# Cross attention with two score slots a batch, and a feed-forward that turns values still carrying their rounding constant

## The chip, the cores and the metric

The kernel runs on one core of a Trainium2 chip. A core has a matrix engine (TensorE, PE in the profile; its weight loads are listed apart as PEld), a vector engine (VectorE, DVE), an activation engine (ScalarE, ACT), a general engine (GpSimd, POOL) and a sync engine (SyncE, SP) that here only issues DMAs. Each engine runs its own list of instructions in order; the engines wait for one another through semaphores. SBUF is the working memory and PSUM the memory into which PE writes.

The metric is the device time of one launch in microseconds (us). Lower is better.

## The reference

A decoder of two layers over x [32, 256, 256] (32 batches of 256 rows of 256 values), each step followed by a residual sum and a layer norm:

```python
x = layernorm(x + linear attention(x))
x = layernorm(x + cross attention 0(x, ctx, mask))   # x and ctx are normalised first, keys are masked
x = layernorm(x + expert attention(x))
x = layernorm(x + state space scan(x))
x = layernorm(x + cross attention 1(x, ctx, ctx))    # biases on q, k, v; no mask
x = layernorm(x + quantised feed-forward(x))
```

A cross attention has 16 heads of 16 values and 77 context rows: q from x, k and v from ctx [32, 77, 256], softmax over q k / 4, times v, a projection. The feed-forward quantises each row of its input to whole numbers within +-127 (scale 127 / max|x|) and its weights to -1, 0 and 1 (scale 1 / mean|w|), computes silu(gate) * up with 1024 inner values, quantises that again by row, and projects down.

## The kernel before

Six stages run one after the other, each with its own buffers and semaphores. The change touches three: `cross_attention` (called as xa0 with `normed` and `masked`, and as xa1 with neither) and `bit_ffn`.

**Cross attention.** One loop turn handles four batches. The order of every engine's work in a batch is written out by hand in its function `batch(this, nxt, after, before, two_before)`: while the scores of batch `this` are worked on, the context of the next batch is turned and projected, x of the one after is turned, and the outputs of the ones before are projected and normalised. A batch has four units u = 0 to 3: C = 2 halves of the heads (c = u // 2) times T = 2 tiles of 128 rows (t = u % 2). A unit holds 8 heads x 77 scores = 616 values on 128 partitions. For each unit:

- PE `scores` (L650) writes the scores to one of two PSUM buffers `pS[u % 2]`. It contracts over 64 partitions, with four heads side by side in `kheads` (308 columns), so two matmuls on two halves of the partitions make a unit. In xa0 a matmul with `fill_row` (L648) comes ahead of each for the mask.
- DVE `unit` takes the maximum (L962) and subtracts it (L963, `low`), ACT `expo` makes the exponential (L785, `e`), DVE `sums` adds up and inverts (L970, L971), POOL `divide` multiplies (L881, `prob`).
- PE `turn` transposes five 128x128 blocks (L661), ACT `turned` copies them out (L790).

For each half c, PE `values` (L676) multiplies with `v_blocks` and ACT `copy_o` (L795) copies the result; `project_out` (L686) follows, then DVE `residual` (L997) and `moments` (L1003, L1007), POOL `rstd_of`, and ACT `finish` (L838). For the batch ahead: PE `turn_x` (L604), ACT `copy_x` (L748), PE `turn_ctx` (L614), ACT `copy_ctx` (L755), PE `project_kv` (L622, L625) and `project_q` (L635), ACT `copy_k`, `copy_v`, `copy_q` (L769, L777, L762), POOL `spread_k` (L889, L891). xa0 also has DVE `norm_stats` (L945 to L955, and in every second batch two mask operations, L950 and L951), POOL `norm_scale` (L871 to L874) and ACT `norm_apply` (L829, L830). SP issues the loads, the stores, and `spread_v`: 12 small DMAs that lay v out in `v_blocks`.

The order before:

- PE: scores 2, turn_ctx, turn 0, values of before c=1, project_kv, project_q, scores 3, turn 1, scores of next 0, turn 2, half of project_out, values c=0, scores of next 1, other half of project_out, turn_x, turn 3.
- DVE: unit 2, sums 1, sums 2, norm_stats, unit 3, unit 0 of next, sums 3, sums 0 of next, unit 1 of next, residual, moments.
- ACT: copy_ctx, turned 0, expo 2, copy_o c=1, finish, copy_k, copy_v, copy_q, turned 1, expo 3, turned 2, expo 0 of next, norm_apply, copy_o c=0, copy_x, turned 3, expo 1 of next.

**Feed-forward.** A slot handles one tile of 128 rows; 64 slots. DVE in slot n: `hidden(n)` (L2656 product, L2659 maximum, L2636 and L2637 scale), `quantize_h(n-1)` (L2665), `residual(n-2)` (L2673 to L2678), `quantize_x` in odd slots (L2649) and `top_x` in even ones. ACT multiplies and adds the constant 12582912, which rounds (`scale_h` L2557, `scale_x`); DVE takes the constant off again, clamps and writes bf16; PE transposes in bf16 (L2521, L2514); ACT copies out.

Of the kernel before, what the change touches and what calls it, by code (L numbers as in the profile page):

```python
# [8 lines left out]
bf16 = mybir.dt.bfloat16  # L9
# [405 lines left out]
def cross_attention(nc, name, x_in, x_out, ctx_d, wq_d, wkv_d, wo_d, bo_d, ident_d, heads_d,  # L415
# [15 lines left out]
    with Stage(nc, name) as st:  # L431
        sb, ps, sem = st.sb, st.ps, st.sem
        ident = sb("ident", [P, P])
        head_of = sb("head_of", [P, HB])
        wq = sb("wq", [P, C, D])
# [9 lines left out]
        pick = sb("pick", [P, 3])  # L445
        fill = sb("fill", [P, 1])
# [25 lines left out]
        kheads = sb("kheads", [P, 2, C, HB * CTX])  # L472
# [18 lines left out]
        pS = [ps(f"pS{k}", [P, 2, 512]) for k in range(2)]  # L491
# [49 lines left out]
        def _(sp):  # L541
# [50 lines left out]
        def _(pe):  # L592
            def turn_x(j, b, before):
# [5 lines left out]
                if before is not None:  # L599
                    pe.wait_ge(oT_ready, 2 * number(*before) + 1)  # L600
                for c in range(C):
# [27 lines left out]
            def project_q(j, b, before):  # L629

                if before is not None:
                    pe.wait_ge(oT_ready, 2 * number(*before) + 2)
# [6 lines left out]
            def scores(j, b, u):  # L639
                p, c, t = b % 2, u // T, u % T  # L640
                if u == 0:
                    pe.wait_ge(kheads_ready, number(j, b) + 1)
                    pe.wait_ge(q_copied, number(j, b) + 1)
                pe.wait_ge(low_ready, unit_number(j, b, u) + 1)
                for h in range(2):
                    rows = slice(h * P // 2, (h + 1) * P // 2)
                    if masked:
                        pe.matmul(pS[u % 2][:, h, 0:HB * CTX], ones[rows, :],  # L648
                                  fill_row[rows, b, :].unsqueeze(1).broadcast_to([P // 2, HB, CTX]), start=True, stop=False)
                    last = pe.matmul(pS[u % 2][:, h, 0:HB * CTX], qT[rows, p, c, t * P:(t + 1) * P], kheads[rows, p, c, :],  # L650
                                     start=not masked, stop=True)
# [12 lines left out]
            def values(j, b, c, nxt):  # L664

                if c == 0:
                    pe.wait_ge(k_copied, number(*(nxt if nxt is not None else (j, b))) + 1)
                    pe.wait_ge(v_copied, number(*(nxt if nxt is not None else (j, b))) + 1)
                    pe.wait_ge(v_spread[b % 2], spread * (2 * j) + spread * (b // 2 + 1))
                elif not (type(j) is int and j == 0 and b == 0):  # L670
                    pe.wait_ge(res_added, number(j, b))
                pe.wait_ge(eT_copied, 2 * unit_number(j, b, T * c + T) + 2)
                out = pG[1 - c][:, 0:S]
# [6 lines left out]
            def project_out(j, b, t, ahead):  # L680
                if t == 0:
                    pe.wait_ge(oT_ready, 2 * number(j, b) + 2)
                    if ahead is not None:
                        pe.wait_ge(q_copied, number(*ahead) + 1)
                for c in range(C):
                    last = pe.matmul(pG[0][:, t * D:(t + 1) * D], oT[:, b % 2, c, t * P:(t + 1) * P], wo[:, c, :],  # L686
                                     start=(c == 0), stop=(c == C - 1))
                if t == T - 1:
                    last.then_inc(proj_made, 1)

            def batch(this, nxt, after, before, two_before):

                j, b = this
                scores(j, b, 2)
# [3 lines left out]
                if before is not None:  # L698
                    values(*before, 1, None)
                if nxt is not None:  # L700
                    project_kv(*nxt)
                    project_q(*nxt, before)
                scores(j, b, 3)
                turn(j, b, 1)
                if nxt is not None:
                    scores(*nxt, 0)
                turn(j, b, 2)
                if before is not None:
                    project_out(*before, 0, nxt)
                values(j, b, 0, nxt)  # L710
                if nxt is not None:
                    scores(*nxt, 1)
                if before is not None:
                    project_out(*before, 1, nxt)
                if after is not None:
                    turn_x(*after, this)
                turn(j, b, 3)
# [17 lines left out]
            scores(0, 0, 1)  # L735
            pe.wait_ge(v_copied, 1)
            turn_x(0, 1, None)
            batches(pe, batch)
            values(*last_batch, 1, None)
            project_out(*last_batch, 0, None)  # L740
            project_out(*last_batch, 1, None)

        @block.scalar
        def _(act):
# [35 lines left out]
            def expo(j, b, u):  # L780
                m = unit_number(j, b, u)
                act.wait_ge(low_ready, m + 3)
# [10 lines left out]
            def copy_o(j, b, c):  # L793
                act.wait_ge(oT_made, 2 * number(j, b) + (c + 1))
                act.activation(oT[:, b % 2, c, :], pG[1 - c][:, 0:S], ACT.Copy).then_inc(oT_ready, 1)  # L795

            def batch(this, nxt, after, before, two_before):
# [5 lines left out]
                if before is not None:  # L803
                    copy_o(*before, 1)
                if two_before is not None:
                    finish(*two_before)
                if nxt is not None:
                    copy_k(*nxt)
                    copy_v(*nxt)
                    copy_q(*nxt)  # L810
                turned(j, b, 1)
                expo(j, b, 3)
                turned(j, b, 2)
                if nxt is not None:
                    expo(*nxt, 0)
                if after is not None and normed:
                    norm_apply(*after)
                copy_o(j, b, 0)
                if after is not None:
                    copy_x(*after)  # L820
                turned(j, b, 3)
                if nxt is not None:
                    expo(*nxt, 1)

# [42 lines left out]
        def _(pool):  # L867
# [16 lines left out]
            def spread_k(j, b):  # L884
# [5 lines left out]
                for c in range(C):  # L890
                    last = pool.tensor_tensor(kheads[:, p, c, :].rearrange("p (h s) -> p h s", h=HB),  # L891
                                              kT[:, p, c, :].unsqueeze(1).broadcast_to([P, HB, CTX]),
                                              head_of[:, :].unsqueeze(2).broadcast_to([P, HB, CTX]), ALU.mult)
# [7 lines left out]
            def batch(this, nxt, after, before, two_before):  # L901
                divide(*this, 1)
                divide(*this, 2)
                if nxt is not None:
                    spread_k(*nxt)
                if after is not None and normed:
                    norm_scale(*after)
                divide(*this, 3)
                if nxt is not None:
                    divide(*nxt, 0)  # L910
                    add_bias(*nxt)
                if before is not None:
                    rstd_of(*before)
# [13 lines left out]
            pool.wait_ge(w_loaded, 16 * len(loads))  # L927
            if bv_d is not None:
# [6 lines left out]
            divide(0, 0, 0)  # L935
            batches(pool, batch, link)
            rstd_of(*last_batch)

        @block.vector
        def _(dve):  # L940
# [16 lines left out]
            def unit(j, b, u):  # L957

                dve.wait_ge(scores_made, unit_number(j, b, u) + 1)
                s = pS[u % 2][:, :, 0:HB * CTX].rearrange("p g (h s) -> p g h s", h=HB)  # L960
                m = top[:, u % 2, :].rearrange("p (g h) -> p g h", g=2)
                link(dve.tensor_reduce(m, s, AX.X, ALU.max))  # L962
                dve.tensor_tensor(low[:, u % 2].rearrange("p (g h s) -> p g h s", g=2, h=HB), s,  # L963
# [1853 lines left out]
```

## Time and profile before

| what | us |
|---|---|
| median of 3 runs (4072.92 to 4078.64) | 4076.7 |
| the profiled execution | 4074.91 |
| its span | 4073.1 |
| of it xa0 | about 337 to 851 |
| of it xa1 | about 3184 to 3674 |
| of it the feed-forward | about 3674 to 4073 |

The profiled execution is 1.8 us below the median of the runs. Over the span PE is busy 83%, DVE 79%, ACT 67%, POOL 65%. An engine's busy time counts its instructions, not its waits. A row of the timeline gives start, busy time, engine, line, operation, what is written and read, shape, a count where several were merged, and in brackets the idle time before it with what ended that. A row of a stretch gives its bounds and length, then for PE, PEld, DVE, ACT and POOL the busy time and the count of instructions, then PE's granted clock (1.00 is full), the busy share of the DMA engines and GB/s.

### The profile page before, as it was taken

Reading aid. Unit: us, or ns where it says so; the run is one execution under the profiler, and the core shown is the slowest. Engines: PE = TensorE matmul, PEld = TensorE weight load, DVE = VectorE, ACT = ScalarE, POOL = GpSimd, SP = SyncE. Lnnn points to the kernel's source line nnn. Section 1 sums busy time; section 2 is a strip of 40 time slices with the busy share of each in tenths; the row PEclk is TensorE's granted clock in tenths of the full one; section 3 lists DMA queues with packets and bytes.
Section 4 is the critical chain, followed back from the end, with each engine's and each line's share of the span. In section 5 each row is a group of like instructions: output and inputs, shape, how many; then the busy total and the mean of one; then the engine's idle time right before and its main releaser. Section 6 shows DMA issues by size and latency. Waiting matters only on the chain. (4 is left out here: it accounts for less than half of the span.)

```text
span 4073.1 us, 72788 instructions
## 1 busy us (share of the span) xinstructions
PE 3400.3 (83%) x22080; PEld 2446.4 (60%) x22080; DVE 3229.4 (79%) x5435; ACT 2743.3 (67%) x5009; POOL 2665.4 (65%) x2794
## 2 busy tenths in 40 slices
PE   8996999979853888898888888888888799994666
PEld 5664666676431677677666776676667466662333
DVE  5665888844593899898989989898998477877988
ACT  2223777733473888788888888788887366664766
POOL 1223667710292899898988989898999266562555
PEclk9998999979976999999999999999999799997999
DMA  2111221151122111111111111111111121112110
GB/s 62 52 57 51 49 49 46 47 117 28 28 63 59 45 47 55 52 53 54 55 47 52 54 47 54 50 56 52 50 47 46 44 52 49 47 38 73 53 47 32
DMA packets 284837, 209.71 MB, mean 51 GB/s; under 512 B 131208, under 2 KB 249544, under 8 KB 284504
## 3 DMA queue, kind: packets, MB, share of 16 engines
q1 hardware_dynamic: 284504, 205.72, 18.3%
q8 instruction: 154, 2.52, 0.3%
q14 instruction: 179, 1.47, 0.1%
HBM read 149.18 MB, written 51.41 MB: 49 GB/s over the span
## 5 line engine op out<-in xcount | busy, mean ns | idle before, releaser
L2167 POOL TENSOR_TENSOR ma_ch<-ma_h,ma_crep 128x512 f32<-128x512 f32 x1024 | 1378.1, 1366 | 175.1 <-DVE ma_h L2269 165.6
L2269 DVE TENSOR_TENSOR_SCAN ma_h<-ma_a,ma_pbu 128x512 f32<-128x512 f32 x1024 | 1215.1, 1207 | 195.3 <-PE ma_pbu L1855 132.3
L1855 PE MATMUL ma_pbu<-ma_ident,ma_bu 128*128 128x128 f32 x4096 | 657.3, 284 | 223.5 <-DVE ma_h L2269 182.9
L1855 PEld LDWEIGHTS ma_pbu<-ma_ident,ma_bu 128*128 128x128 f32 x4096 | 475.0, 144 | 463.2 <-DVE ma_h L2269 359.4
L2057 ACT ACTIVATE ma_a<-ma_dt,ma_A 128x510 f32<-128x510 f32 x1024 | 652.4, 715 | 1.1 <-issue 1.1
L1864 PE MATMUL ma_py<-ma_ident,ma_ch 128*128 128x128 f32 x4096 | 623.6, 278 | 0.8 <-POOL ma_ch L2167 0.8
L1864 PEld LDWEIGHTS ma_py<-ma_ident,ma_ch 128*128 128x128 f32 x4096 | 494.3, 145 | 11.1 <-issue 9.8
L2048 ACT ACTIVATE ma_bu<-ma_uT,ma_b_t 128x512 f32<-128x512 f32 x736 | 478.1, 716 | 23.4 <-PE ma_pbu L1855 21.4
L881 POOL TENSOR_TENSOR xa_prob<-xa_e,xa_rec_head 128x616 f32<-128x616 f32 x256 | 306.4, 1217 | 284.3 <-DVE xa_rec_head L971 284.2
L962 DVE TENSOR_REDUCE xa_top<-xa_pS 128x8 f32<-128x616 f32 x256 | 200.9, 785 | 138.7 <-PE xa_pS L650 135.6
L785 ACT ACTIVATE xa_e<-xa_low 128x616 f32<-128x616 f32 x256 | 184.9, 722 | 92.5 <-DVE xa_low L963 92.5
L790 ACT ACTIVATE xa_eT<-xa_pE 128x384 f32<-128x384 f32 (+1 forms) x512 | 197.9, 446 | 43.4 <-PE xa_pE L661 43.2
L963 DVE TENSOR_TENSOR xa_low<-xa_pS,xa_top 128x616 f32<-128x616 f32 x256 | 204.6, 799 | 8.8
L970 DVE TENSOR_REDUCE xa_esum<-xa_e 128x8 f32<-128x616 f32 x256 | 197.5, 772 | 4.8 <-ACT xa_e L785 4.8
L650 PE MATMUL xa_pS<-xa_kheads,xa_qT 64*128 64x308 f32 x1024 | 188.7, 444 | 11.0 <-POOL xa_kheads L891 9.0
L661 PE MATMUL xa_pE<-xa_ident,xa_prob 128*128 128x128 f32 x1280 | 191.7, 281 | 6.8 <-POOL xa_prob L881 6.7
L661 PEld LDWEIGHTS xa_pE<-xa_ident,xa_prob 128*128 128x128 f32 x1280 | 139.4, 141 | 63.8 <-issue 45.2
L337 POOL TENSOR_TENSOR la_veps<-la_mv,la_eps 128x2 f32<-128x2 f32 x32 | 6.3, 197 | 250.2 <-DVE la_mv L370 250.2
L2235 DVE SCALAR_TENSOR_TENSOR ma_xc<-ma_pm,ma_conv,ma_xc 128x510 f32<-128x510 f32 (+2 forms) x192 | 140.2, 730 | 24.9 <-ACT ma_xc L1993 22.5
L1541 POOL MEMSET scatter_eps<- 128x4 f32 x1 | 0.1, 102 | 239.2 <-POOLq L40 239.2
L676 PE MATMUL xa_pG<-xa_eT,xa_v_blocks 128*32 128x256 f32 x2048 | 139.6, 385 | 1.5 <-ACT xa_eT L790 1.5
L686 PE MATMUL xa_pG<-xa_wo,xa_oT 128*128 128x256 f32 x512 | 137.9, 392 | 1.0 <-ACT xa_oT L795 1.0
(314 smaller groups left out, 7370.9 us busy)
## 6 DMA issues: line engine op xcount, KB each, us to landing
ma_crep<-ma_ct_dram SPq DMA_DIRECT2D x256, 256.0 KB, 3.3
xa_x<-act SPq DMA_DIRECT2D x64, 256.0 KB, 2.9
act<-xa_y SPq DMA_DIRECT2D x64, 256.0 KB, 2.1
la_x<-in_x SPq DMA_DIRECT2D x32, 256.0 KB, 2.7
act<-la_y SPq DMA_DIRECT2D x32, 256.0 KB, 2.2
ea_x<-act SPq DMA_DIRECT2D x32, 256.0 KB, 11.7
act<-ea_x SPq DMA_DIRECT2D x32, 256.0 KB, 4.0
ma_x<-act SPq DMA_DIRECT2D x16, 512.0 KB, 4.6
```

The source lines that it names most:

```text
L661: last = pe.transpose(pE[h][:, i, :], prob[:, u % 2, k * P:(k + 1) * P], ident[:, :])
L790: act.activation(eT[:, u // T, halves[h][0]:halves[h][-1] + 1, u % T, :], pE[h][:, 0:len(halves[h]), :], ACT.Copy).then_inc(eT_copied, 1)
L881: pool.tensor_tensor(prob[:, u % 2, 0:HC * CTX].rearrange("p (h s) -> p h s", h=HC), e[:, u % 2].rearrange("p (h s) -> p h s", h=HC), rec_ ...
L962: link(dve.tensor_reduce(m, s, AX.X, ALU.max))
L963: dve.tensor_tensor(low[:, u % 2].rearrange("p (g h s) -> p g h s", g=2, h=HB), s, m.unsqueeze(3).broadcast_to([P, 2, HB, CTX]), ALU.subtr ...
L970: link(dve.tensor_reduce(esum[:, u % 2, :], e[:, u % 2].rearrange("p (h s) -> p h s", h=HC), AX.X, ALU.add))
L1855: last = pe.transpose(pbu[c % 2][:, t * P:(t + 1) * P], bu[:, s % 2, t, c * P:(c + 1) * P], ident[:, :])
L1864: last = pe.matmul(py[:, t, c * P:(c + 1) * P], ch[:, s % 2, c, t * P:(t + 1) * P], ident[:, :], start=(s == 0 and c == 0), stop=(s == N - ...
L2048: last = act.activation(bu[:, s % 2, t, :], uT[:, par, t, :], ACT.Copy, scale=b_t[:, par, t, s:s + 1])
L2057: act.activation(a[:, s % 2, c, :].rearrange("p (b t) -> p b t", b=GB)[:, :, 1:S], dt[:, par, c, :].rearrange("p (b t) -> p b t", b=GB)[:, ...
L2167: pool.tensor_tensor(ch[:, s % 2, c], h[:, s % 2, c], crep[:, s % 4, :], ALU.mult).then_inc(multiplied, 1)
L2269: dve.tensor_tensor_scan(out=h[:, s % 2, c, :], data0=a[:, s % 2, c, :], data1=pbu[c % 2][:, :], initial=0.0, op0=ALU.mult, op1=ALU.add).t ...
```

## The change

In `cross_attention` the scores go in two slots a batch, one for each half c of the heads and both row tiles at once, into one PSUM buffer of four banks. The contraction is over 32 partitions (two heads side by side, 154 columns), so eight matmuls fill a slot. All four orders are rewritten, with other waits. In `bit_ffn` PE transposes the f32 values that still hold the constant, ACT takes it off in the copy from PSUM, and `quantize_x` and `quantize_h` go.

```diff
-        pS = [ps(f"pS{k}", [P, 2, 512]) for k in range(2)]
+        pS = ps("pS", [P, 4, T, 256])
-        kheads = sb("kheads", [P, 2, C, HB * CTX])
+        kheads = sb("kheads", [P, 2, C, 2 * CTX])
 # SP
                 sp.wait_ge(v_copied, n + 1)
+                if n >= 2:
+                    sp.wait_ge(oT_made, 2 * n - 2)
...
+                if n + 1 < B:
+                    spread_v(n + 1)
                 if n >= 2:
                     store(n - 2)
-                if n + 1 < B:
-                    spread_v(n + 1)
 # PE
+            def scores(j, b, c):
+                if not (type(j) is int and j == 0 and b == 0 and c == 0):
+                    pe.wait_ge(low_ready, unit_number(j, b, T * c))
+                for t in range(T):
+                    if masked:
+                        for g in range(4):
+                            rows = slice(32 * g, 32 * g + 32)
+                            pe.matmul(pS[:, g, t, 0:2 * CTX], ones[rows, :], fill_row[rows, b, :]...)
+                    for g in range(4):
+                        rows = slice(32 * g, 32 * g + 32)
+                        last = pe.matmul(pS[:, g, t, 0:2 * CTX], qT[rows, p, c, t * P:(t + 1) * P], kheads[rows, p, c, :], ...)
+            def batch(this, nxt, after, before, two_before):        # PE, the new order
+                scores(this, 1); turn_ctx(nxt); turn(this, 0); project_kv(nxt); turn(this, 1)
+                project_q(nxt)       # waits for res_added of two_before
+                values(before, 1)    # waits for k_copied and v_copied of nxt
+                scores(nxt, 0)
+                values(this, 0)      # waits for oT_ready of before c=1: both halves now use pG[1]
+                turn(this, 2); project_out(before); turn(this, 3); turn_x(after)
 # ACT, the new order; (n) where normed, (p) where not
+                copy_ctx(nxt); turned 0; expo 2; copy_k(nxt); copy_v(nxt); turned 1; expo 3; copy_q(nxt)
+                copy_o(before, 1); copy_o(this, 0); turned 2; (n) norm_apply(after); expo 0 of nxt
+                (p) finish(two_before); (p) expo 1 of nxt; turned 3; copy_x(after)
+                (n) expo 1 of nxt; (n) finish(two_before)
 # POOL, the new order
+                spread_k(nxt); (n) norm_scale(after); divide 2; divide 3; rstd_of(two_before)
+                add_bias(nxt); divide 0 of nxt; divide 1 of nxt
 # DVE, the new order
+                unit 2; unit 3; (n) norm_stats(after); sums 2; sums 3; moments(two_before)
+                unit 0 of nxt; unit 1 of nxt; sums 0 of nxt; residual(before); sums 1 of nxt
 # bit_ffn
-                act.activation(hT[:, k % 2], ph[:, :, :], ACT.Copy).then_inc(hT_copied, 1)
+                act.activation(hT[:, k % 2], ph[:, :, :], ACT.Copy, bias=-ROUND).then_inc(hT_copied, 1)
-                dve.tensor_scalar(hq[:, k % 2], hr[:, k % 2], ROUND, 127.0, ALU.subtract, ALU.min).then_inc(hq_ready, 1)
-                dve.tensor_scalar(xq[:, m % 2], xr[:, :, :], ROUND, 127.0, ALU.subtract, ALU.min).then_inc(xq_ready, 1)
-        px, ph, pd = ps("px", [P, T, C, P], bf16), ps("ph", [P, IC, P], bf16), ps("pd", [P, 512])
+        px, ph, pd = ps("px", [P, T, C, P]), ps("ph", [P, IC, P]), ps("pd", [P, 512])
 # its setup: DVE clips three weight blocks (was: clip, then clip to bf16), ACT takes the constant off
+                dve.tensor_scalar(w, w, ROUND - 1.0, ROUND + 1.0, ALU.max, ALU.min).then_inc(w_clipped, 1)
+                last = act.activation(q, w, ACT.Copy, bias=-ROUND)
```

The orders are shown in short form here, one call after the other. The setup of the attentions gains a few small additions on DVE (`head_of_two`, `rest_pick`).

## Rows read from the trace of the kernel before

**Rows 1.** Busy time of each engine, four batches of xa1 and of xa0.
```profile
3408.98:3465.82 56.84, 55.31 (x409) 36.62 (x409) 45.47 (x89) 38.32 (x100) 34.37 (x45) 1.00 0.19 48
560.55:619.90 59.35, 56.58 (x441) 37.30 (x441) 52.39 (x121) 45.25 (x114) 41.73 (x65) 1.00 0.21 49
```
**Rows 2.** Waits, xa1 from 3252 to 3638: us in total, times, longest.
```profile
DVE xa_top L962 <- PE xa_pS L650: 61.7, 51, 2.2
```
**Rows 3.** Timeline, xa1, the steps of one batch on PE and ACT.
```profile
3410.39 0.66 ACT L748 ACTIVATE xa_xT<-xa_pG 128x256 f32<-128x256 f32 x2 [1.77 <-PE xa_pG L604]
...
3412.18 0.38 ACT L755 ACTIVATE xa_cT<-xa_pG 128x77 f32<-128x77 f32 x2
...
3412.38 1.09 PE L676 MATMUL xa_pG<-xa_eT,xa_v_blocks 128*32 128x256 f32 x16
3412.41 0.81 ACT L790 ACTIVATE xa_eT<-xa_pE 128x384 f32<-128x384 f32 x2
...
3413.40 0.97 PEld L622 LDWEIGHTS xa_pG<-xa_cT,xa_wkv 128*128 128x128 f32 x8 [0.41 <-issue]
...
3413.93 0.72 ACT L785 ACTIVATE xa_e<-xa_low 128x616 f32<-128x616 f32 x1 [0.71 <-DVE xa_low L963]
...
3414.81 1.08 ACT L838 ACTIVATE xa_y<-xa_r,xa_shift,xa_rstd 128x256 f32<-128x256 f32 x2
...
3415.01 1.70 PEld L635 LDWEIGHTS xa_pG<-xa_xT,xa_wq 128*128 128x128 f32 x8
...
3415.80 0.53 ACT L769 ACTIVATE xa_kT<-xa_pG,xa_bqk 128x77 f32<-128x77 f32 x2
...
3417.04 0.30 PEld L650 LDWEIGHTS xa_pS<-xa_kheads,xa_qT 64*128 64x128 f32 x4 [0.33 <-issue]
...
3417.15 0.84 ACT L762 ACTIVATE xa_qT<-xa_pG,xa_bq 128x256 f32<-128x256 f32 x2 [0.56 <-PE xa_pG L635]
...
3417.76 0.53 PEld L661 LDWEIGHTS xa_pE<-xa_ident,xa_prob 128*128 128x128 f32 x5 [0.42 <-issue]
```
**Rows 4.** Costliest groups of the page: busy, mean ns, idle before.
```profile
L881 POOL TENSOR_TENSOR xa_prob<-xa_e,xa_rec_head 128x616 f32<-128x616 f32 x256 | 306.4, 1217 | 284.3 <-DVE xa_rec_head L971 284.2
...
L963 DVE TENSOR_TENSOR xa_low<-xa_pS,xa_top 128x616 f32<-128x616 f32 x256 | 204.6, 799 | 8.8
```
**Rows 5.** Timeline, xa0, the steps that only it has.
```profile
562.06 1.02 ACT L748 ACTIVATE xa_xT<-xa_pG,xa_norms 128x256 f32<-128x256 f32 x2 [0.75 <-PE xa_pG L604]
...
564.22 0.74 ACT L755 ACTIVATE xa_cT<-xa_pG,xa_norms 128x77 f32<-128x77 f32 x2
...
570.87 0.20 POOL L871 TENSOR_TENSOR xa_n_neg<-xa_n_mv,xa_minus_one 128x3 f32<-128x3 f32 x1
...
572.23 0.20 POOL L874 TENSOR_TENSOR xa_n_shift<-xa_n_neg,xa_n_rstd 128x3 f32<-128x3 f32 x1
...
574.21 1.08 ACT L829 ACTIVATE xa_xn<-xa_x,xa_n_shift,xa_n_rstd 128x256 f32<-128x256 f32 x2
...
581.98 0.76 DVE L945 BATCH_NORM_STATS2 xa_n_stats<-xa_x 128x6 f32<-128x256 f32 x2
...
584.34 0.14 DVE L955 BATCH_NORM_AGGREGATE xa_n_mv<-xa_n_stats 77x2 f32<-77x6 f32 x1
```
**Rows 6.** Timeline, xa0, SP's queue: the twelve issues of one spread_v.
```profile
568.00 10.21 SPq L564 DMA_DIRECT2D xa_v_blocks<-xa_v  x12
```
**Rows 7.** Busy time of each engine, feed-forward.
```profile
3745.00:4050.00 305.00, 209.15 (x1452) 109.50 (x1449) 276.22 (x613) 211.93 (x250) 158.31 (x305) 0.98 0.14 45
```
**Rows 8.** Timeline, feed-forward, the operations that go.
```profile
3908.11 0.67 DVE L2665 TENSOR_SCALAR ff_hq<-ff_hr 128x1024 bf16<-128x1024 f32 x1
...
3908.70 0.48 DVE L2673 SCALAR_TENSOR_TENSOR ff_r<-ff_pd,ff_fd,ff_x 128x256 f32<-128x256 f32 x1
3908.84 0.45 PEld L2521 LDWEIGHTS ff_ph<-ff_identb,ff_hq 128*128 128x128 bf16 x8 [1.74 <-DVE ff_hq L2665]
...
3909.90 0.43 DVE L2649 TENSOR_SCALAR ff_xq<-ff_xr 128x512 bf16<-128x512 f32 x1
```

More of the change, by code:

```diff
@@ L627, in project_kv, with project_q @@
                 last.then_inc(kv_made, 1)
-            def project_q(j, b, before):
-                if before is not None:
-                    pe.wait_ge(oT_ready, 2 * number(*before) + 2)
+            def project_q(j, b, two_before):
+                if two_before is not None:
+                    pe.wait_ge(res_added, number(*two_before) + 1)
                 for f in range(C):
@@ L637, in project_q @@
                 last.then_inc(q_made, 1)
-            def scores(j, b, u):
-                p, c, t = b % 2, u // T, u % T
-                if u == 0:
+            def scores(j, b, c):
+                p = b % 2
+                if c == 0:
                     pe.wait_ge(kheads_ready, number(j, b) + 1)
                     pe.wait_ge(q_copied, number(j, b) + 1)
-                pe.wait_ge(low_ready, unit_number(j, b, u) + 1)
-                for h in range(2):
-                    rows = slice(h * P // 2, (h + 1) * P // 2)
+                if not (type(j) is int and j == 0 and b == 0 and c == 0):
+                    pe.wait_ge(low_ready, unit_number(j, b, T * c))
+                for t in range(T):
                     if masked:
[L648 to L651, printed above, removed]
+                        for g in range(4):
+                            rows = slice(32 * g, 32 * g + 32)
+                            pe.matmul(pS[:, g, t, 0:2 * CTX], ones[rows, :],
+                                      fill_row[rows, b, :].unsqueeze(1).broadcast_to([32, 2, CTX]), start=True, stop=False)
+                    for g in range(4):
+                        rows = slice(32 * g, 32 * g + 32)
+                        last = pe.matmul(pS[:, g, t, 0:2 * CTX], qT[rows, p, c, t * P:(t + 1) * P], kheads[rows, p, c, :],
+                                         start=not masked, stop=True)
                 last.then_inc(scores_made, 1)
@@ L678, in values, with project_out @@
                 last.then_inc(oT_made, 1)
[L680 to L689, printed above, removed]
+            def project_out(j, b, ahead):
+                pe.wait_ge(oT_ready, 2 * number(j, b) + 2)
+                if ahead is not None:
+                    pe.wait_ge(q_copied, number(*ahead) + 1)
+                for t in range(T):
+                    for c in range(C):
+                        last = pe.matmul(pG[0][:, t * D:(t + 1) * D], oT[:, b % 2, c, t * P:(t + 1) * P], wo[:, c, :],
+                                         start=(c == 0), stop=(c == C - 1))
+                last.then_inc(proj_made, 1)
             def batch(this, nxt, after, before, two_before):
                 j, b = this
-                scores(j, b, 2)
+                scores(j, b, 1)
                 if nxt is not None:
@@ L802, in batch @@
                 expo(j, b, 2)
[L803 to L806, printed above, removed]
                 if nxt is not None:
@@ L809, in batch @@
                     copy_v(*nxt)
-                    copy_q(*nxt)
                 turned(j, b, 1)
                 expo(j, b, 3)
+                if nxt is not None:
+                    copy_q(*nxt)
+                if before is not None:
+                    copy_o(*before, 1)
+                copy_o(j, b, 0)
                 turned(j, b, 2)
+                if after is not None and normed:
+                    norm_apply(*after)
                 if nxt is not None:
                     expo(*nxt, 0)
-                if after is not None and normed:
-                    norm_apply(*after)
-                copy_o(j, b, 0)
+                if two_before is not None and not normed:
+                    finish(*two_before)
+                if nxt is not None and not normed:
+                    expo(*nxt, 1)
+                turned(j, b, 3)
                 if after is not None:
                     copy_x(*after)
-                turned(j, b, 3)
-                if nxt is not None:
+                if nxt is not None and normed:
                     expo(*nxt, 1)
+                if two_before is not None and normed:
+                    finish(*two_before)
             def norm_apply(j, b):
@@ L907, in batch @@
                     norm_scale(*after)
+                divide(*this, 2)
                 divide(*this, 3)
+                if two_before is not None:
+                    rstd_of(*two_before)
                 if nxt is not None:
+                    add_bias(*nxt)
                     divide(*nxt, 0)
-                    add_bias(*nxt)
-                if before is not None:
-                    rstd_of(*before)
+                    divide(*nxt, 1)
             def rstd_of(j, b):
@@ L2395, in bit_ffn @@
         ident = sb("ident", [P, P])
-        identb = sb("identb", [P, P], bf16)
         ones = sb("ones", [P, P])
@@ L2518, in turn_h @@
                 k = tile[1]
-                pe.wait_ge(hq_ready, count(tile))
+                pe.wait_ge(hr_ready, count(tile))
                 for c in range(IC):
-                    last = pe.transpose(ph[:, c, :], hq[:, k % 2, c * P:(c + 1) * P], identb[:, :])
+                    last = pe.transpose(ph[:, c, :], hr[:, k % 2, c * P:(c + 1) * P], ident[:, :])
                 last.then_inc(hT_made, 1)
@@ L2682, in slot @@
                     hidden(n)
-                if n_1 is not None:
-                    quantize_h(n_1)
                 if n_2 is not None:
                     residual(n_2)
-                if odd and n3 is not None:
-                    quantize_x(n3)
                 if not odd and n4 is not None:
```

133 lines of the change are left out of this document (64 added, 69 removed).

## The prediction

> **What bounds the kernel now.** I read three views: the busy time of stretches, the waits, and the timeline of one batch. The stages run one after the other, so each of the three that change is judged by itself. A batch of xa1 takes 14.21 us (56.84 / 4) and PE is busy 13.83 of it; a batch of xa0 takes 14.84 and PE is busy 14.15. DVE is busy 11.37 and 13.10, ACT 9.58 and 11.31 [rows 1]. So PE's queue is the bound in both attentions, though DVE looks nearly as full. What the waits add: in 386 us of xa1, 27.2 batches, DVE waited 61.7 us, 2.27 a batch, for the scores [rows 2]. Part of PE's time is no work: a scores slot (3417.04 to 3417.76, 0.72 us) is followed by 0.42 and preceded by 0.33 of idle weight loading, put down to issue [rows 3]. In the feed-forward DVE is the bound: 276 of 305 us, ACT 212, PE 209 [rows 7].
>
> **Feed-forward.** quantize_h goes: it is busy 0.67, but the next instruction starts 0.59 later (3908.11 to 3908.70), and the 0.59 is what DVE's queue loses. quantize_x is busy 0.43; less the same 0.08 of overlap, 0.35. Two tiles have two of the first and one of the second: 2 x 0.59 + 0.35 = 1.53, times 32 pairs 49 us [rows 8]. This holds while DVE stays the bound. The transposes become f32: eight bf16 loads take 0.45 [rows 8], five f32 ones 0.53 [rows 3], so eight take 0.86. Two tiles add 2 x 0.41 and four more for x 0.2, 1.0 us. PE then works 209 / 305 x 10.9 + 1.0 = 8.5 us of a pair that shrinks from about 10.9 to 9.4; ACT stays at 7.6 (212 / 305 x 10.9). Neither ends last. The longer transpose is hidden too: it no longer waits for a DVE pass that ended 1.74 us late [rows 8]. If that cover were gone, 0.41 a tile, 26 us, would be lost. ACT's copies with the constant taken off, from f32 PSUM, are not in the trace; at 0.1 more or less each they lie in ACT's 1.8 us of slack. The setup loses three DVE passes and gains three on ACT that start as soon as each block is clipped; the trace of before has no such ACT pass, and I take 2 us of gain, with -2 to +4 as bounds from three 128x2048 passes priced as three to four 128x1024 ones of 0.67. Sum for the stage: 51 us, bounds 25 to 55.
>
> Here the Trainium skill would price it otherwise. The trace first: the f32 transpose of 128 columns takes 0.107, the bf16 one 0.056 [rows 3, 8], twice. FP8 and Floating Point Precision (TensorE Precision Notes) says that true f32 takes four passes through the array. By that rule eight would take 1.8 us and PE some 10.8 us a pair, and the loop would gain some 3 us. The trace speaks against the rule for transposes; I keep 0.86.
>
> **xa1.** Removed: two of four scores slots and six changes of tile shape (twelve before, six after). The new slot has eight matmuls of 154 columns on 32 partitions. A 256-column f32 load-and-multiply step takes 0.213 (1.70 / 8), so 154 columns take 0.128; there are two steps a matmul. Before, two 64-partition matmuls of 308 columns, four steps of 0.257, fitted in 0.72: two abreast and 0.2 for the change [rows 3]. No row shows four 32-partition tiles abreast, but values runs 16 steps of 0.213 on four column tiles in 1.02 (3412.38 to 3413.40), four abreast [rows 3]. Bounds: four abreast 16 x 0.128 / 4 + 0.2 = 0.71; none abreast 2.25. I take 0.75, nearest to the values row. PE's work falls by about 4 x 0.72 - 2 x 0.75 = 1.4 plus some 1 us of changes, to 11.5: PE no longer fills the batch. DVE's own work and overhead is 14.21 - 2.27 = 11.9. What is late next is a ring through ACT and PE, walked with t = 0 at the end of copy_x. Where ACT's next copy is ready, it starts 0.1 before the busy time of the last would end (y is busy 1.08, kT starts 0.99 later), so each step counts 0.1 less.
>
> - turn_ctx: two loads, and 0.44 as between q's last load and ACT's start on q (3416.71, 3417.15): copy_ctx starts at 0.6, ends at 0.95 (0.38).
> - project_kv starts at 1.1 and takes 1.6 (3413.40 to 3415.01); turn 1 0.53; project_q starts at 3.2 and is there 2.14 later, at 5.4 (3415.01, 3417.15). ACT meanwhile has copy_k, copy_v, turned 1 and expo 3 done by 5.1.
> - copy_q 0.84: 6.2. Beside it PE does values of before (to 6.2). scores of next: 7.05. values c=0 is at ACT 1.19 after it starts (1.09 and a wait of 0.1): 8.3.
> - ACT: copy_o 0.3, turned 2 0.7, expo 0 0.62, finish 0.99, expo 1 0.62, turned 3 0.7, copy_x 0.66: 12.9.
>
> All rows of this walk are [rows 3]. The measured periods hold about 0.1 over a plain one for the loop turn, so 13.0 against 14.21: 1.2 x 32 = 39 us. DVE waits inside this ring, at the sums of unit 3 (expo 3 sits behind turned 1) and the sums of 0 and 1 of next; its 11.9 do not end last. Bounds: 11.9 (73 us) and, with a slot of 2.25, 14.5 (-9 us).
>
> **xa0.** Here expo 1 and finish come after copy_x, and norm_apply joins ACT's ring. From the start of copy_ctx: it takes 0.74, project_kv starts at 0.85, project_q at 3.0 and is there at 5.15; copy_q to 5.9, values of before to 6.0; the scores slot has eight short bf16 matmuls more, I take 0.85, to 6.9; values at ACT 8.1. Then copy_o 0.3, turned 2 0.7, norm_apply 1.5 (1.08 and half as much for the context), expo 0 0.62, turned 3 0.7, copy_x 0.92, expo 1 0.62, finish 0.99: 14.4 [rows 3, 5]. In every second batch the mask makes a second ring longer: a DVE pass of a unit is 0.80 [rows 4], so from the end of expo 1 sums 0.95, two units 3.15, norm_stats with the mask 2.5 (581.98 to 584.48), norm_scale 1.56 (570.87 to 572.43), divide 2 1.22, turn 2 0.55, then turned 2 to expo 1 as above, 5.1: 15.0 [rows 3 to 5]. Moving norm_scale ahead of divide 2 on POOL is what brings this about. The mean is 14.7 against 14.84: 4 us. Bounds: DVE's idle is 1.74 a batch, of which 0.6 is overhead as in xa1 (2.84 idle, 2.27 waited) [rows 1, 2], so at best 13.7, 36 us; at worst 15.2, -12 us. On SP the twelve issues of spread_v take 10.21 [rows 6] and now come ahead of store and the load of x. With the other four or five issues of about 0.4 SP needs 12.3 of 14.7: x of the batch after next lands about as norm_stats asks for it. I count nothing, and price a miss in the third rival. The new wait for oT_made looks back two batches and is long over. kheads is half as large, off the rings.
>
> **Sum.** 51 + 39 + 4 = 94, less 1 for the added setups: 4074.9 - 93 = 3982 by the profiled execution, 1.8 more by the median: 3984.
>
> The Trainium skill's TensorEngine Tiling (Key Properties) says that changing the tiling mode drains the engine. The 0.33 and 0.42 of idle beside each scores slot agree [rows 3]. By this rule alone, six changes fewer at 0.2 each, PE would give back 1.2 us a batch; the ring above shows that this is not what ends last.
>
> **Rivals.**
>
> 1. DVE becomes the bound in both attentions: the ACT ring has slack that I don't see, for instance since ACT's waits overlap its pipeline. 11.9 and 13.7: 51 + 73 + 36 = 160, 3917. For it: DVE has the largest plain sum. Against: expo 3 behind two steps on PE. Chance 0.13.
> 2. The 32-partition matmuls do not run abreast: 2.25 a slot, 1.5 us on each ring, and 0.4 for the mask in xa0. xa1 14.5, xa0 16.6: +9 and +56, less 51: 4091, slower than before. It decides from a slot of about 2.2 us. Against: two tiles abreast in the trace. Chance 0.05.
> 3. xa0 gets slower by its second ring or by x landing late: 15.2, 12 us more instead of 4 less: 4000. Chance 0.17.
> 4. PE or ACT ends last in the feed-forward. The 0.41 a tile uncovered, 26 us less gained: 4010, chance 0.07. Or an f32 transpose costs four bf16 ones here (0.224): 2 x 1.34 + 0.67 = 3.35 on PE's 7.5, 10.8 a pair, 46 us less gained: 4030, chance 0.03; against it stands the 0.107 of the attention's rows [rows 3]. This second case is what the Trainium skill's page on precision, above, would have.
> 5. The attentions hardly move, since copy and PE alternate on more waits than I walked: 14.1 and 14.8, only the feed-forward pays: 4076.7 - 55 = 4022. Chance 0.1.
>
> **How the numbers follow.** The forecast has 0.45, with its own range 3962 to 4005. The range 3915 to 4030 leaves out rival 2, what lies under rival 1 and what lies over rival 4. What a measurement tells from no change is about 8 us. Faster 0.94, same 0.02, slower 0.04: slower is rival 2 with a little less than its whole weight.
>
> **What would show it.** Feed-forward: hidden starts at a spacing of 9.4 us for two tiles, and DVE's waits stay under 15 us. xa1: a period of 13.0, a scores slot near 0.75, DVE idle at expo 3 and at expo 1, PE busy near 11.5 to 12. xa0: batches of 14.4 and 15.0 in turn, t2's transposes in mask batches right after a divide. Wrong would be: scores slots above 1 us, attention periods under 12.5 (ring too long) or over 14, or ACT or PE without idle time in the feed-forward.

## The result, and the profile after

The changed kernel takes 4017.1 us (median of 4 runs, 4015.1 to 4018.2) against 4076.6 for the one before, measured beside it: ratio 0.9856, 95% interval 0.9842 to 0.9871. It is faster by 59.5 us, where 93 were forecast. The profiled span is 4016.0.

Taken from the issue of each stage's identity load on SP's queue to the next stage's, the stages of one profiled execution last, in us:

| stage | before | after | change | forecast |
|---|---|---|---|---|
| xa0 | 514.0 | 547.1 | +33.1 | -4 |
| expert attention | 392.3 | 393.9 | +1.6 | 0 |
| scan | 1940.3 | 1943.1 | +2.8 | 0 |
| xa1 | 490.4 | 445.5 | -44.9 | -39 |
| feed-forward | 398.7 | 349.1 | -49.6 | -51 |

The periods, as spacing of the residual additions (of `hidden` for two tiles), go from 14.87 to 15.92 in xa0, 14.21 to 12.69 in xa1 and 10.93 to 9.49 in the feed-forward. So two stages did what was forecast, and one went the other way. The miss of 33 us (36 by the profiled executions) is xa0's 37, 4 of the two stages that nothing was done to and 1 of the feed-forward, less the 6 that xa1 gave beyond its forecast (37 + 4 + 1 - 6).

Busy time of the engines after: start:end and length in us, then PE, PEld, DVE, ACT and POOL with their instructions, TensorE's granted clock, DMA share, GB/s. The first row is xa0, the second four batches of xa1, the third the feed-forward.
```profile
420.00:820.00 400.00, 333.20 (x3364) 246.64 (x3363) 324.01 (x754) 284.64 (x707) 250.80 (x401) 0.96 0.19 45
3300.00:3350.80 50.80, 48.20 (x473) 36.96 (x473) 45.80 (x89) 38.59 (x102) 32.61 (x45) 1.00 0.23 56
3710.00:4000.00 290.00, 239.21 (x1592) 155.82 (x1590) 259.88 (x578) 230.42 (x276) 145.93 (x332) 1.00 0.16 50
```
In xa0 no engine is near full: PE is busy 83%, where it was 95% [rows 1]. The waits of xa0, 420 to 820, show what holds it (us in total, times, longest):
```profile
SPq L565 <- PE xa_pG L691: 88.1, 25, 5.1
...
DVE xa_n_stats L963 <- DMA xa_x<-act: 34.8, 24, 2.5
...
POOL xa_n_neg L886 <- DVE xa_n_mv L973: 37.3, 24, 3.1
...
PE xa_pE L673 <- POOL xa_prob L896: 39.8, 39, 2.8
```
Line 565 is `sp.wait_ge(oT_made, 2 * n - 2)`, the change's new wait. It holds SP for 3.5 us a batch. Behind it in SP's queue stand the twelve issues of spread_v, the store and the load of x. VectorE waits for that x in 24 of 25 batches, POOL's norm_scale waits for VectorE, divide 2 stands behind norm_scale, and PE waits for divide 2. In the kernel before, the wait for x came to 1.2 us in the same 400. One turn of it on the timeline (start, duration, idle before and its releaser in brackets):
```profile
597.94 0.46 SPq L548 DMA_DIRECT2D xa_x<-act  x1
...
598.29 0.38 ACT L787 ACTIVATE xa_v<-xa_pG 77x256 f32<-77x256 f32 x1
...
600.21 1.09 PE L691 MATMUL xa_pG<-xa_eT,xa_v_blocks 128*32 128x256 f32 x16
...
600.74 0.75 DVE L963 BATCH_NORM_STATS2 xa_n_stats<-xa_x 128x6 f32<-128x256 f32 x2 [2.23 <-DMA xa_x<-act]
...
601.78 10.24 SPq L568 DMA_DIRECT2D xa_v_blocks<-xa_v  x12
...
602.71 0.19 POOL L886 TENSOR_TENSOR xa_n_neg<-xa_n_mv,xa_minus_one 128x3 f32<-128x3 f32 x1 [2.81 <-DVE xa_n_mv L973]
...
605.60 0.76 PE L673 MATMUL xa_pE<-xa_ident,xa_prob 128*128 128x128 f32 x5 [2.42 <-POOL xa_prob L896]
...
612.18 0.40 SPq L558 DMA_DIRECT2D act<-xa_y  x1
...
612.63 0.46 SPq L548 DMA_DIRECT2D xa_x<-act  x1
```
v is copied and ready at 598.7, but the spread starts at 601.78, just after values c=1 (600.21 to 601.3). So the load of x comes at 612.63 and not some 3 us earlier.

xa1, by contrast, follows the walk of the prediction closely. PE and ACT, one batch, to be set against [rows 3]:
```profile
3403.73 0.67 ACT L758 ACTIVATE xa_xT<-xa_pG 128x256 f32<-128x256 f32 x2
3404.84 0.36 ACT L765 ACTIVATE xa_cT<-xa_pG 128x77 f32<-128x77 f32 x2 [0.44 <-PE xa_pG L621]
...
3407.62 1.89 PE L642 MATMUL xa_pG<-xa_xT,xa_wq 128*128 128x256 f32 x8
...
3410.62 0.58 PEld L662 LDWEIGHTS xa_pS<-xa_kheads,xa_qT 32*128 32x128 f32 x16 [0.57 <-issue]
3411.36 0.61 PEld L691 LDWEIGHTS xa_pG<-xa_eT,xa_v_blocks 128*32 128x32 f32 x16 [0.16 <-issue]
...
3412.55 0.38 ACT L805 ACTIVATE xa_oT<-xa_pG 128x256 f32<-128x256 f32 x1 [1.54 <-PE xa_pG L691]
```
From the end of copy_x at 3404.40: project_q at 3.22 (walked 3.2), scores of next at 6.22 (6.2), the slot 0.74 long (0.75), values at ACT at 8.15 (8.3).

### The profile page after: what moved, and what is told of

Its sections match the earlier page's. It is cut to its first block and busy times, and to the rows that moved or that the text cites. A ratio compares the mean times of both kernels' runs of the same rounds, so it can differ in the third digit from the quotient of the medians.

```text
span 4016.0 us, 75319 instructions
## 1 busy us (share of the span) xinstructions
PE 3333.1 (83%) x23360; PEld 2509.1 (62%) x23360; DVE 3179.1 (79%) x5339; ACT 2747.2 (68%) x5012; POOL 2608.2 (65%) x2794
## 5 line engine op out<-in xcount | busy, mean ns | idle before, releaser
L673 PEld LDWEIGHTS xa_pE<-xa_ident,xa_prob 128*128 128x128 f32 x1280 | 152.7, 146 | 102.6 <-issue 73.1
L2201 POOL TENSOR_TENSOR ma_dt<-ma_dt,ma_gT 128x512 f32<-128x512 f32 x64 | 103.9, 1624 | 50.0 <-DVE ma_gT L2281 50.0
L1921 PE MATMUL ma_pm<-ma_wout,ma_one_av 128*128 128x256 f32 x512 | 133.9, 386 | 0.0
```

Source lines behind the costliest of these rows:

```text
L673: last = pe.transpose(pE[h][:, i, :], prob[:, u % 2, k * P:(k + 1) * P], ident[:, :])
```

## The experiments

A kernel's stage length and period are those of its profiled execution, as above; its ratio is to the kernel before on the same chip (median 4074 to 4079).

### One part alone

**old_xa0**: `cross_attention(nc, "xa0", ...)` calls the function of the kernel before; xa1 and the feed-forward are the new ones.
```diff
-        cross_attention(nc, "xa0", ...)
+        cross_attention_old(nc, "xa0", ...)
```


> The changed kernel with xa0 (the normed cross attention) as it was before; xa1 and the feed-forward as changed. Theory (the loss is all in xa0, 547 us against 514): xa0 about 514 us again, the whole about 4017 - 33 = 3984. Rival (part of the loss is made elsewhere, in the 4 us by which the two unchanged stages grew, or xa0's length hangs on what follows): xa0 514 but the whole over 3990.

Measured 3978.3 us, ratio 0.9764 (0.9748 to 0.9780), xa0 513.3, xa1 445.4, feed-forward 349.0. The 39 us gained on the changed kernel are, in the profiled executions, xa0's 33.8 and 4.5 in the two stages behind it, which fall back to 392.2 and 1940.3. The theory holds: 3978 is under the rival's 3990. Other kernels here show 390 to 394 and 1939 to 1944 for these two with nothing changed in them, so their 4 us are not explained.

**ffn_only**: the kernel before with the new `bit_ffn`.
```diff
-def bit_ffn(...):   # of before
+def bit_ffn(...):   # of after
```


> The kernel before with the feed-forward of the change alone. Theory: the stages are independent, so the feed-forward takes about 349 us instead of 399 and the whole about 4076.7 - 50 = 4027. Rival (part of the 50 us comes from a state left by the attentions): less than 45 us gained.

Measured 4025.9, ratio 0.9878 (0.9861 to 0.9894); the stage 348.7, 50.0 less. The gains of the stages add: these 50.0 and xa1's 44.9 make 94.9, and old_xa0, which has both, is 94.9 shorter than the kernel before by the spans.

### Which wait delays x

**four_v_blocks**: v_blocks has four buffers, so SP's wait looks back four batches.
```diff
-        v_blocks = sb("v_blocks", [P, 2, C, HB, 2, W])
+        v_blocks = sb("v_blocks", [P, 4, C, HB, 2, W])
-                if n >= 2:
-                    sp.wait_ge(oT_made, 2 * n - 2)
+                if n >= 4:
+                    sp.wait_ge(oT_made, 2 * n - 6)
```


> The changed kernel with four v_blocks buffers instead of two, so that SP's wait for oT_made looks four batches back. Theory (SP's new wait, 88 us in 25 batches of xa0, makes spread_v late, with it the load of x, and norm_stats waits for x): SP's wait at that line and DVE's wait for xa_x are gone, xa0's period falls from 15.9 to about 14.7, xa0 by some 35 us, the whole to about 3982. Rival (POOL's order, norm_scale ahead of divide 2, or ACT's, sets the period by itself): the waits go, but the period stays above 15.4 and the whole above 4000. xa1 stays at 12.7, as its x is wanted later.

Measured 4004.3, ratio 0.9823 (0.9807 to 0.9840), xa0 530.4: 16.7 us of the 33. The waits of this kernel in the same 400 us:
```profile
SPq L568 <- ACT xa_v L787: 52.1, 25, 3.5
SPq L558 <- ACT xa_y L853: 32.1, 26, 2.4
...
DVE xa_n_stats L963 <- DMA xa_x<-act: 5.9, 18, 1.2
```
SP now waits for v, which it needs, and for y, whose finish stands at the end of ACT's batch. The waits for x all but go (5.9 us of 34.8), yet the gain is half of the 35 us that the theory had: the period is 15.4 and the kernel over 4000, as the rival said.

**load_first**: with two blocks, SP issues the load of x ahead of the store of y.
```diff
-                if n >= 2:
-                    store(n - 2)
                 if n >= 1 and n + 3 < B:
                     sp.wait_ge(res_added, n)
                     load_x((n + 3) % 4, n + 3)
+                if n >= 2:
+                    store(n - 2)
```


> The changed kernel with SP issuing the load of x ahead of the store. Theory (norm_stats waits for x): x lands 0.5 to 1 us earlier in each batch, xa0's period falls by 0.3 to 0.5, xa0 by 8 to 15 us, the whole to about 4005. Rival (POOL's or ACT's order alone): the whole stays at 4017.

Measured 4009.8, ratio 0.9842 (0.9826 to 0.9859), xa0 540.7: 6.4 us less, a little under the 8 to 15 expected. VectorE still waits 25.7 us for x in the same 400.

**both_dma**: the two edits together.
```diff
+        four v_blocks, and load_x ahead of store
```


> The changed kernel with both hindrances of the x load gone: value blocks of four batches (no wait of SP for oT_made of the batch before) and the load of x issued ahead of the store of y. Theory A (the first cross attention is slow only because x lands late): no wait of VectorE for x is left, the period falls from 15.43 (four value blocks alone) and 15.76 (load first alone) to 14.9 or less, the stage to about 515 us, the kernel to 3986. Rival B (what is left is the order of the work within the batch): VectorE still no longer waits for x, but the period stays at 15.3 to 15.4, the stage at 526 to 529, the kernel at 3999 to 4003. With A and B in equal parts the stage would be at 520.

Measured 3994.3, ratio 0.9791 (0.9774 to 0.9807), xa0 530.5 (period 15.34), no wait for x left on VectorE. The stage stands where four_v_blocks had it. Theory A falls, and Rival B's forecast is the nearer one for the stage: taking the late x away gives 16.6 us, and the other half of the loss is elsewhere. (The 16.6 are a net gain: the section on xa0 below shows that more batches ran with a lower TensorE clock once x came in time.) (Of the 10 us between the two medians none is in xa0; the scan and xa1 are 6.0 shorter in this profile.)

### Which order in the batch

**pool_order**: as both_dma, and
```diff
+                divide(*this, 2)
                 if after is not None and normed:
                     norm_scale(*after)
-                divide(*this, 2)
```


> As both_dma, and POOL takes divide 2 ahead of norm_scale (four small operations, 1.4 us in a row). This is the place that the prediction named. Rival B2 (norm_scale's wait for the statistics and its 1.4 us delay divide 2, turn 2 and its copy): period 0.5 to 1.0 us shorter than in both_dma, the stage 16 to 32 us less. Rival B1: the same time within 0.2 us a batch, because TensorE waits for the projections' copies and not for the probabilities.

Measured 3988.3, ratio 0.9779 (0.9762 to 0.9795), xa0 520.7: 9.8 us less. That is more than the 6 (0.2 a batch) that B1 allows and less than the 16 at the low end of B2's gain.

**pool_only**: the same edit on the changed kernel itself.

> The changed kernel with one edit: POOL takes divide 2 ahead of norm_scale. SP's wait for oT_made and the late x stay. In the changed kernel POOL waited 37.3 us in 24 batches for the statistics of the next x, with divide 2 queued behind. Theory C (the late x reaches the probabilities only because norm_scale stands ahead of divide 2; the two causes are coupled): more than the 9.8 us that this order gave once x came in time, 15 to 25 us, the stage at 522 to 532, the kernel at 3992 to 4002. Rival P (the two causes add): 10 us, the stage at 537, the kernel at 4007. Rival N (norm_apply of the late x sets the pace by itself through ScalarE, wherever POOL has norm_scale): within 3 us, the stage at 544 to 550, the kernel at 4014 to 4020.

Measured 4004.1, ratio 0.9820 (0.9803 to 0.9836), xa0 536.9: 10.2 us less. Rival P: the gain is the same with the late x and without it.

**act_order**: as both_dma, with finish and expo 1 ahead of the last turned copy.
```diff
                     expo(*nxt, 0)
+                finish(*two_before); expo(*nxt, 1)
                 turned(j, b, 3); copy_x(*after)
-                expo(*nxt, 1); finish(*two_before)
```


> As both_dma, and on ScalarE of the first cross attention finish (1.09 us) and the exp of unit 1 (0.72 us) stand ahead of the last turned copy, as they do in the second one, so that copy_ctx follows copy_x at once. Rival B1 (these 1.8 us between copy_x and copy_ctx hold up turn_ctx's copy, hence kv, the keys and the next scores): the period falls against both_dma by 0.5 to 1.0 us, the stage by 16 to 32 us. Rival B2 (POOL's norm_scale ahead of divide 2 sets the pace): no change within 0.2 us a batch, or slower, since the last turned copy and copy_x now start up to 1.8 us later.

Measured 4018.4, ratio 0.9849 (0.9832 to 0.9865), xa0 555.0: 24.5 us more. B1 is refuted, and the order that suits xa1 costs xa0 0.8 us a batch. Not all of that is the order itself: 16 of 25 batches ran with a stretch below TensorE's full clock, 13 in both_dma, and the others took 14.9 us, against 14.6 to 14.9 in both_dma. PE waited 53.8 us for copy_x (25 times, 2.2 at most) where it waited 14.7 in both_dma.

**act_pool**: both orders.

> As both_dma, with ScalarE's order and POOL's order both changed as in the two kernels before. If each of the two orders holds a part of the loss, the gains add up and the stage comes to 500 us or less (period 14.4, the kernel at 3971); if one ring alone sets the pace, it is as fast as the better of the two; if neither does, it stands where both_dma does and something that none of the four touches (the order of VectorE or TensorE) keeps the period.

Measured 4021.7, ratio 0.9855 (0.9839 to 0.9872), xa0 551.8. None of the cases fits; with ACT's order the gain of POOL's is 3 us. Here 17 of 25 batches had a stretch below the full clock.

### Which engine sets the pace

**scalar_probe** and **vector_probe**: old_xa0 with an idle operation added to one engine, in each batch of xa1 and each tile of the feed-forward.
```diff
+ (ACT, behind expo 0) act.activation(probe, wo, ACT.Copy)            # 128x512
+ (ACT, each tile)     act.activation(probe, ident twice, ACT.Copy)   # 128x256
```
```diff
+ (DVE, behind sums 3) dve.tensor_reduce(probe, wo, ALU.add)           # 128x512
+ (DVE, each tile)     dve.tensor_reduce(probe, ident twice, ALU.add)  # 128x256
```


> As old_xa0, with a ScalarE copy of 128x512 from SBUF into a buffer nobody reads (about 0.6 us) in each batch of the second attention, behind expo 0 of the next batch, and one of 128x256 (about 0.35 us) in each tile of the feed-forward; both are extra work. Theory R (ScalarE's ring sets the pace of the second attention): period 12.69 + 0.5 to 0.6 = 13.2 to 13.3. Rival D (VectorE): 12.7 to 12.8. Feed-forward, theory V (VectorE is the bound): the pair stays at 9.46 within 0.1. Rival S (ScalarE): 9.46 + 0.7 = 10.1 to 10.2.

> As old_xa0, with a VectorE sum of 128x512 from SBUF (about 0.65 us) into a buffer nobody reads in each batch of the second attention, behind the sums of unit 3, and one of 128x256 (about 0.35 us) in each tile of the feed-forward; both are extra work. Theory R: VectorE has some 0.6 us of waits a batch to take it up, so the period is 12.7 to 12.9. Rival D: 12.69 + 0.65 = 13.3. Feed-forward, theory V: 9.46 + 0.7 = 10.1 to 10.2 a pair. Rival S: 9.5 to 9.6.

What they cost, first in the kernel with ACT's, then in the one with DVE's (groups of xa1 and of the feed-forward: count, busy, mean ns):
```profile
L1450 ACT ACTIVATE xa_probe<-xa_wo 128x512 f32<-128x512 f32 x24 | 15.1, 630 | 0.0
...
L3236 ACT ACTIVATE ff_probe<-ff_ident 128x256 f32<-128x256 f32 x55 | 22.6, 410 | 0.0
```
```profile
L1620 DVE TENSOR_REDUCE xa_probe<-xa_wo 128x8 f32<-128x512 f32 x25 | 15.9, 634 | 0.0
...
L3325 DVE TENSOR_REDUCE ff_probe<-ff_ident 128x2 f32<-128x256 f32 x50 | 19.3, 386 | 0.0
```

| operation added | xa1 period, 12.69 | feed-forward pair, 9.46 |
|---|---|---|
| ACT, 0.63 and 0.41 a tile | 13.21 (+0.52) | 9.46 (0) |
| DVE, 0.63 and 0.39 a tile | 12.85 (+0.16) | 10.18 (+0.72) |

Theory R holds in xa1: the same 0.63 us costs 0.52 on ACT and 0.16 on DVE, which had the rest idle. Theory V holds in the feed-forward, sharply: ACT's is free, DVE's is paid nearly in full. Ratios 0.981 (0.979 to 0.983) and 0.983 (0.981 to 0.985).

**late_finish**: as pool_order, with finish one batch later, between ACT's two copies of oT, in both attentions; the store follows.
```diff
                     copy_o(*before, 1)
+                if three_before is not None:
+                    finish(*three_before)
                 copy_o(j, b, 0)
```


> As pool_order (four value blocks, x loaded ahead of the store, divide 2 ahead of norm_scale), and in both cross attentions finish (two activations, 1.1 us) runs one batch later, in ScalarE's wait of 1.5 us between the two copies of oT; the store follows a batch later. Theory R (a ring through ScalarE and TensorE sets the pace of both): the ring loses about 1.0 us. Second attention: from 12.69 down to where VectorE ends last, 12.69 less its 0.6 us of waiting a batch, 12.1 to 12.2, the stage about 428 us; first attention from 14.96 to 14.0 to 14.3, about 495 us; the kernel about 3945. Rival D (VectorE already sets the pace of the second attention): 12.6 to 12.7 as before, only the first may gain. Rival Q (the ring does not run through finish, ScalarE only waits longer elsewhere): neither changes by more than 0.2 us a batch.

Measured 3963.5, ratio 0.9720 (0.9702 to 0.9737), the fastest kernel here: 53.6 us under the changed one, and 14.7 under old_xa0 by the medians of two sets of runs. xa0 506.1 (period 14.51) is under the old one at last; xa1 435.8 (12.38). Less than Theory R gave in both: 0.31 a batch in xa1 and 0.45 in xa0 (14.96 in pool_order) of the 1.0 taken off ACT. In xa1 the busy times of that kernel offer a reason:
```profile
3260.00:3580.00 320.00, 312.79 (x3053) 238.79 (x3050) 295.62 (x570) 249.15 (x647) 211.18 (x286) 1.00 0.23 55
```
PE is busy 98% of it: the bound that the change had removed seems to be back, at 12.4. No run added work to PE to test this.

## Why the prediction was right or wrong

**Feed-forward: right.** 51 forecast, 49.6 measured, 50.0 alone. DVE was the bound and still is (the probe), PE is busy 7.8 of a pair of 9.49 (239.21 / 290 x 9.49; 8.5 forecast) and ACT 7.5 (7.6). The eight f32 transposes of a tile, in the group of their weight loads over 3710 to 4000, are busy 56.8 / 62 = 0.92 us:
```profile
L2544 PEld LDWEIGHTS ff_ph<-ff_ident,ff_hr 128*128 128x128 f32 x494 | 56.8, 140 | 6.0
```
0.86 was priced. The four passes that the Trainium skill's FP8 and Floating Point Precision (TensorE Precision Notes) gives for true f32, 1.8 us by an estimate, did not come; the row decides. ACT's copies that take the constant off cost nothing more: the mean copy into `hT` takes 1.01 us, where it took 1.02 (1010 and 1019 ns, group means of the two kernels).

**xa1: right in mechanism, 6 us short.** The slot (0.74 for 0.75) and the ring of ACT and PE are as walked; the ring is 12.6 to 12.7 for 13.0, a few steps 0.1 earlier each. Rival 1 (DVE) is refuted for xa1 by the probes, rival 2 by the slot, rival 5 by the period. What the walk did not see is how close PE was behind: its work is 12.05 a batch (48.20 / 4) and not 11.5, which would explain why late_finish got only 0.31.

**xa0: wrong.** Forecast -4, measured +33. The steps that failed:

- "The new wait for oT_made looks back two batches and is long over." It was not over in any of the 25 batches seen. spread_v of batch n needs values c=1 of batch n - 2, and in the new order PE does that in the batch in which v of n is copied, 2 us behind it (600.21 against 598.29). Looking back two batches in numbers was no slack in time. The sentence had no row behind it.
- "x of the batch after next lands about as norm_stats asks for it. I count nothing". With the 12.3 us of issues in a batch of 14.7, SP had 2.4 us to spare, and the wait took 3.5. x came 1.4 us late a batch on average (34.8 / 24). Price by both_dma: 16.6 us net. The third rival had the mechanism; its 15.2 was too low, since it priced either miss and both came, with a third, the clock.
- "Moving norm_scale ahead of divide 2 on POOL is what brings this about." Right in mechanism; that the size fits is partly luck. 0.6 in every second batch, 0.3 on average, 10 us, was in the sum; 9.8 and 10.2 measured. But the batches with mask operations, at the full clock, took 14.72 in both_dma and 14.40 in pool_order: 0.32 and not 0.6. The other half of the 9.8 comes with the clock: 10 of 25 batches had a stretch below the full clock, where both_dma had 13.
- The first ring of 14.4 is right at TensorE's full clock and was walked for nothing else: the sum put a fall of the clock at nothing, without a word. In pool_order, which has neither late x nor second ring, this costs 20 us (520.7 against 514 - 4 - 10 = 500). No run isolates this cause, but the batches of one trace, sorted by clock, show it.

The granted clock over 420 to 820 was 1.00 before, and 0.96, 0.94, 0.95 and 0.97 in the changed kernel, both_dma, pool_order and late_finish. It was lowest, 0.91 and 0.92, in act_order and act_pool, and 0.98 in pool_only. In pool_order two batches follow each other, the first with a stretch at the lower clock (0.50, 1.2 GHz), the second without. The three rows of stretches are PE just before the fall, at the lower clock, and in the second batch:
```profile
598.00:601.00 3.00, 1.57 (x11) 1.19 (x12) 2.42 (x5) 3.00 (x8) 2.28 (x3) 1.00 0.16 15
...
601.60:605.00 3.40, 3.40 (x12) 2.51 (x11) 3.32 (x10) 2.28 (x7) 1.14 (x3) 0.50 0.71 172
...
616.00:630.00 14.00, 12.10 (x130) 8.83 (x129) 12.62 (x30) 10.70 (x28) 9.91 (x16) 1.00 0.17 44
```
```profile
601.49 1.81 PE L632 MATMUL xa_pG<-xa_wkv,xa_cT 128*77 128x256 f32 x4
603.10 1.27 PE L673 MATMUL xa_pE<-xa_ident,xa_prob 128*128 128x128 f32 x5
604.17 2.31 PE L642 MATMUL xa_pG<-xa_xT,xa_wq 128*128 128x256 f32 x8
...
617.48 1.03 PE L632 MATMUL xa_pG<-xa_wkv,xa_cT 128*77 128x256 f32 x4
618.34 0.71 PE L673 MATMUL xa_pE<-xa_ident,xa_prob 128*128 128x128 f32 x5
618.89 1.89 PE L642 MATMUL xa_pG<-xa_xT,xa_wq 128*128 128x256 f32 x8
```
From the start of the first to the end of the third, these steps take 4.99 us in the first batch and 3.30 in the second: 1.69 more at the lower clock. That is also what a batch gets longer by. Cut from copy_ctx to copy_ctx on ACT, pool_order's batches fall into two kinds; the first two rows below are batches without the mask operations on DVE, the last two are batches with them:
```profile
599.76:615.75 15.99, 14.56 (x138) 10.74 (x137) 12.73 (x30) 11.40 (x30) 9.99 (x16) 0.89 0.26 50
...
630.30:644.60 14.30, 12.94 (x138) 9.68 (x138) 12.55 (x30) 11.23 (x30) 9.94 (x16) 1.00 0.24 53
...
644.60:660.57 15.97, 14.33 (x136) 10.64 (x135) 13.22 (x32) 11.35 (x29) 10.01 (x16) 0.89 0.20 43
...
705.15:719.48 14.33, 12.54 (x134) 9.20 (x133) 13.00 (x32) 11.24 (x30) 9.91 (x16) 1.00 0.20 48
```
Of the 25 batches from 419.54 to 794.59, the 10 with a mean clock of 0.89 took 15.96 to 15.99, with mask operations or without, and the 15 at 1.00 took 14.30 to 14.55, 14.35 on average; 14.4 was walked. So the clock costs 1.6 us in 10 of 25 batches, 0.65 a batch, an estimated 21 us over the stage's 32: the 20 us missing. Sorted in the same way, the changed kernel has such a stretch in 8 of 25 batches and both_dma in 13, in every batch without mask operations. Removing the late x therefore gave less than it would have at one and the same clock.

Before the clock fell, PE was busy 1.57 of 3 us, waiting for copy_x and for divide 0; the kernel before has PE busy 95% in xa0 [rows 1]. Why the clock fell in some batches and not in others is not shown. The Trainium skill's TensorE: Matmul & The Clock Gate (Terms) has a rule for the cost, the time at the lower clock times one less the share of the clock left. This trace agrees: 1.69 us lost, and the stretch of 3.40 at 0.50 gives 1.70 by the rule.

**The sum.** It was helped by its bounds and by the other two stages: 4017 lies in the range, near its end, and the likeliest case's own range (3962 to 4005) missed it. The whole came out faster only because the 94.5 us of xa1 and the feed-forward outweigh a stage whose sign was wrong.

## What to carry to other kernels

When a DMA is moved past others, or a wait is put ahead of them, walk the issuing queue as a ring of its own, with the times at which its conditions come true: "two batches back" is an index, and here the event it names fell 2 us too late, 3.5 us a batch. To learn which engine sets a stage's pace, add the same idle operation to one engine at a time: it separated 0.52 from 0.16 and 0.72 from 0 in one run each. And where a change frees the bound engine, check what it has to be given to keep busy: in xa0, once PE had idle time in each batch, its granted clock fell in many of them, and a batch with such a fall took 1.6 us more.

## What the runs showed of the hardware that was not expected

- TensorE's granted clock fell to 0.50 (601.6 to 605.0 in pool_order) without one long idle stretch: the waits of PE before it were 0.50, 0.84 and 0.24 us, with short work between them. It fell in every second batch of both_dma, and nowhere in the same 400 us of the kernel before.
- 32-partition f32 matmuls of 154 columns run about four abreast: sixteen records in a slot of 0.74 us in xa1. One after the other they would take 16 x 0.128 = 2.05, an estimate from the 256-column step of 0.213 [rows 3].
- Taking a wait away can be paid for with the clock: both_dma has a mean clock of 0.94 though x comes in time, and the changed kernel 0.96 with x late.
